# Which of sixteen states ScalarE, VectorE and GpSimd multiply in a selective scan

## The chip, the cores and the metric

The kernel runs on one core of a Trainium2 chip. The metric is the device time of one execution in microseconds (us), the median of several runs.

## The reference

A convolution and state-space block (layer 0) is followed by attention and a mixture of experts with eight experts (layer 1). Only the scan of layer 0 matters here. For each of two images, four groups of channels and four directions of reading the image (K), with D = 128 channels and N = 16 states on L = 2304 positions:

```
dA = exp(d[..., None] * A)
h = h * dA + (d * u)[..., None] * Bv[:, :, None, :]
y = einsum('bkdn,bkn->bkd', h, Cv)
```

So for each state n the kernel needs, for 128 channels by all positions, the decay exp(d*A_n), the drive du*B_n (B_n is one row, the same for all channels), the recurrence along the positions, and the sum over n of h_n*C_n.

## The kernel before, in words

The phases run one after the other; the scan is `scan_phase` (from L587). The 128 channels lie on the partitions and the positions in the free dimension, in chunks of 768 (WC). There are 8 units (image and group); each has 12 steps (4 directions by 3 chunks), and each step has 16 tiles, one for each state n. Every engine has a program written out by hand for the 192 tiles of a unit, in order of t = 16*step + n; the units 1 to 6 run in a hardware loop. Nothing plans the order at run time: an engine takes its instructions in the order of its program and waits on semaphores.

What happens to the tile of state n:

- The decay is one ScalarE exponential (L834), into a buffer `da` (four of them) in SBUF, for the two soft states into PSUM.
- The drive du*B_n is made in one of three ways, by the list in which n stands. For HARD states TensorE spreads the row B_n over all partitions with two matmuls into PSUM (`spread`, L726), and VectorE multiplies this in place with du (`multiply`, L856). For WARM states ScalarE makes the product: du lies transposed (positions on the partitions), so B_n is a scalar of each partition, and six ACTIVATEs of 128x128 with a scale do it (`heat`, L795, into one of two buffers `warm`); TensorE turns the six blocks back into PSUM (`turn`, L734). For SOFT states (4 and 12) GpSimd multiplies du with a copy of B_n that a DMA has put on all partitions (`drive`, L906).
- VectorE runs the recurrence (`scan`, L877); it carries the state in `h[n]` from step to step.
- GpSimd multiplies h with C_n, which a DMA has put on all partitions (`weigh`, L912, six buffers `hc`), and TensorE adds it up over n in PSUM by two matmuls with the identity, which the profile records as four (`sum_up`, L743), eight tiles behind. ScalarE copies the finished y (L778), and the SP queue stores it.

Three PSUM tiles (`ps_p`, PR = 3) go round in order of place. Sixteen places are for the tiles, and a seventeenth, ahead of state 10 (FLIP), is for the flip: six transposes of the next step's du (L715) and six of its `rows`, the B (L717), which ScalarE copies out (`read_flip`, L785) at n = 11. A place is free when the tile three places earlier has been scanned (for the flip: has been copied); `slot_free` waits for that at the start of every flip, spread and turn, and before the exponential of a soft state. Since the flip has a place of its own, tile 10 waits for the scan of tile 8, 11 for 9, and 13 for 10 (12 takes the flip's place); the other tiles wait for the tile three states earlier.

The orders of the programs around the change: TensorE at t takes the flip (if n = 10), then spread or turn of tile t, then the sum of tile t - 8; the sum of state 0 waits for the copy of y. VectorE at t takes the multiply of tile t if it is HARD, then the scan of tile t - 1. ScalarE at t takes the copy of y (n = 9), `read_flip` (n = 11), then the products of tile t + 2 if that is WARM (`HEAT` = 2), then the exponential of tile t. GpSimd takes the drive three tiles ahead, then the product with C of tile t, which waits for the sum six tiles back. The SP queue issues the loads of the next step at n = 8, between the loads of C, and these are paced by GpSimd's products (six buffers).

The lists themselves are four lines at the top of the file:

```
SOFT = (4, 12)
WARM = (1, 3, 6, 8, 10, 13, 15)
HARD = tuple(n for n in range(N) if n not in SOFT + WARM)
FLIP, HEAT = 10, 2
```

Of the kernel before, what the change touches and what calls it, by code (L numbers as in the profile page):

```python
# [29 lines left out]
STACK = 128  # L30
PIECE = 512
SOFT = (4, 12)
WARM = (1, 3, 6, 8, 10, 13, 15)
HARD = tuple(n for n in range(N) if n not in SOFT + WARM)
NB = WC // 128
FLIP, HEAT = 10, 2
# [550 lines left out]
def scan_phase(nc, P, keep):  # L587
# [3 lines left out]
    with ExitStack() as ctx:  # L591
# [21 lines left out]
        TILES = STEP * N  # L613
        NH, NS, NW = STEP * len(HARD), STEP * len(SOFT), STEP * len(WARM)
        steps = [(p + 2 * r, (NCH - 1 - c if r else c), c == 0, r) for p in range(PAIRS) for r in range(2) for c in range(NCH)]
        hard_at = lambda t: (t // N) * len(HARD) + sum(n in HARD for n in range(t % N))
        soft_at = lambda t: (t // N) * len(SOFT) + sum(n in SOFT for n in range(t % N))
        warm_at = lambda t: (t // N) * len(WARM) + sum(n in WARM for n in range(t % N))
        cool_at = lambda t: t - soft_at(t)
# [80 lines left out]
        def _(pe):  # L700
# [19 lines left out]
            def spread(u, t, first, last):  # L720
                st, n = divmod(t, N)
                if n == 0:
                    pe.wait_ge(dd_here[st % 2], u * (48 * STEP // 2) + 48 * (st // 2) + 48)
                slot_free(u, place(t), first, last)
                for lo, hi in pieces:
                    mm = pe.matmul(ps_p[place(t) % PR][:, lo:hi], keep["b_sel"][:, n, :], cut[st % 2][:, lo:hi], start=True, stop=True)  # L726
                mm.then_inc(spread_done, 1)

            def turn(u, t, first, last):
                slot_free(u, place(t), first, last)  # L730
                w = warm_at(t)
                pe.wait_ge(warm_done, u * NW + w + 1)
                for b in range(NB):
                    mm = pe.transpose(ps_p[place(t) % PR][:, b * 128:b * 128 + 128], warm[w % WR][:, b, :], keep["ident"][:, :])  # L734
                mm.then_inc(turned_done, 1)
# [10 lines left out]
            def unit(u, first, last):  # L746
                for t in range(TILES):
# [6 lines left out]
                    if t % N in HARD:  # L754
                        spread(u, t, first, last)
                    elif t % N in WARM:
                        turn(u, t, first, last)
# [16 lines left out]
        def _(act):  # L774
# [5 lines left out]
            def read_flip(u, st, first):  # L780
                act.wait_ge(flip_full, u * STEP + st + 1)
                if not first or st > 1:
                    act.wait_ge(warm_done, u * NW + (st - 1) * len(WARM))
                place = flip_place(st - 1) if st else flip_place(STEP - 1) - STEP * (N + 1)
# [14 lines left out]
            def unit(u, first, last):  # L799
                for t in range(TILES):  # L800
# [14 lines left out]
                    ahead = t + HEAT  # L815
                    if ahead % N in WARM:
                        if ahead < TILES:
# [1121 lines left out]
```

## Time and profile before

| what | value |
|---|---|
| median of 3 runs | 6382.03 us (6374.76 to 6386.11) |
| profiled execution | 6374.7 us, span 6372.7 us |
| TensorE busy, whole span | 5243.1 us (82%) |
| VectorE busy | 4366.0 us (69%) |
| GpSimd busy | 4197.2 us (66%) |
| ScalarE busy | 3768.5 us (59%) |
| scan (806 to 4120 us) | 3314 us |
| granted clock of TensorE | 0.919 over the span |

Shares of the whole span mix the phases: in the profile's 40 slices VectorE, TensorE and GpSimd stand at 8 or 9 tenths in the scan and fall off behind it, where TensorE alone is busy. The rest of the work is best read in stretches. The chain that ended last, as the page gives it, only covers the experts at the end and says nothing of the scan. Durations in the timelines are those of the records; instructions of one engine overlap by some 0.1 us, so the distance from start to start is the time that one takes from its engine. In the timelines DVE is VectorE, ACT ScalarE, POOL GpSimd, PE TensorE's matmuls, PEld its weight loads and SPq the queue of DMA issues on SP.

### The profile page before, as it was taken

The numbers are of one execution on the slowest core, as the hardware profiler recorded it, in microseconds if no ns is written. First come the engines' busy times: TensorE is split into PE (matmuls) and PEld (weight loads), VectorE is DVE, ScalarE is ACT, GpSimd is POOL, SyncE is SP. The second block draws the span as 40 slices with busy tenths as digits, with TensorE's granted clock in tenths as the row PEclk, the third lists the DMA queues.
The fourth block names the chain that finished last, engine by engine and source line by source line (L and its number), as shares of the span: only waits on it lengthen the run. The fifth ranks groups of instructions, "written<-read, shape, count | busy, mean of one in ns | idle before, by whom it ended". The sixth has DMA issues, their size and how long they took to land. (4 is left out here: it accounts for less than half of the span.)

```text
span 6372.7 us, 85894 instructions
## 1 busy us (share of the span) xinstructions
PE 5243.1 (82%) x22476; PEld 3559.1 (56%) x22476; DVE 4366.0 (69%) x4451; ACT 3768.5 (59%) x8015; POOL 4197.2 (66%) x2811
## 2 busy tenths in 40 slices
PE   4767489999898998998989999845699999956994
PEld 2333255555555555555555555422389999935773
DVE  2566599999999999999999999865231111154332
ACT  2555578788777887877878788635532222232332
POOL 0455689999998999999999999831034444402441
PEclk8888599999999999999999999967799999975996
DMA  3454477777777777777777777664200000012213
GB/s 90 139 188 177 186 238 249 249 241 249 240 248 243 238 248 236 249 249 239 248 236 249 249 243 249 221 220 159 72 3 0 0 0 0 0 52 90 84 58 109
DMA packets 399677, 1073.47 MB, mean 168 GB/s; under 512 B 51470, under 2 KB 94511, under 8 KB 393600
## 3 DMA queue, kind: packets, MB, share of 16 engines
q1 hardware_dynamic: 387808, 1043.07, 49.6%
q0 software_dynamic: 7584, 20.72, 1.0%
q10 hardware_dynamic: 3840, 4.72, 0.3%
q8 instruction: 160, 2.62, 0.2%
q14 instruction: 285, 2.33, 0.1%
HBM read 883.39 MB, written 184.94 MB: 168 GB/s over the span
## 5 line engine op out<-in xcount | busy, mean ns | idle before, releaser
L912 POOL TENSOR_TENSOR scan_hc<-scan_h,scan_c_rep 128x768 f32<-128x768 f32 x1536 | 2743.3, 1826 | 259.7 <-PE scan_ps_y L743 233.5
L743 PE MATMUL scan_ps_y<-scan_hc,keep_ident 128*128 128x512 f32 (+1 forms) x6144 | 2220.8, 489 | 24.4 <-ACT scan_y L778 21.0
L877 DVE TENSOR_TENSOR_SCAN scan_h<-scan_da,scan_h,scan_ps_p 128x768 f32<-128x768 f32 x896 | 1572.8, 1793 | 0.0
L743 PEld LDWEIGHTS scan_ps_y<-scan_hc,keep_ident 128*128 128x128 f32 x6144 | 1067.9, 190 | 827.7 <-issue 744.1
L834 ACT ACTIVATE scan_da<-scan_dd,layer_a_neg 128x768 f32<-128x768 f32 x1344 | 1208.8, 925 | 186.5 <-DVE scan_h L877 180.3
L795 ACT ACTIVATE scan_warm<-scan_du_t 128x128 f32<-128x128 f32 x4032 | 1243.1, 388 | 2.7 <-PE scan_ps_p L734 2.3
L1254 POOL TENSOR_TENSOR attn_e_lo<-attn_e,attn_e_hi 128x384 fp32r<-128x384 f32 x432 | 437.1, 1012 | 769.0 <-DVE attn_e_hi L1245 769.0
L877 DVE TENSOR_TENSOR_SCAN scan_h<-scan_da,scan_ps_p 128x768 f32<-128x768 f32 x448 | 760.7, 1733 | 2.0 <-ACT scan_da L834 2.0
L856 DVE TENSOR_TENSOR scan_ps_p<-scan_ps_p,scan_dd 128x768 f32<-128x768 f32 x672 | 634.1, 944 | 138.6 <-PE scan_ps_p L726 137.6
L1245 DVE CAST attn_e_hi<-attn_e 128x384 fp32r<-128x384 f32 x432 | 165.3, 383 | 713.4 <-ACT attn_e L1233 713.4
L734 PE MATMUL scan_ps_p<-keep_ident,scan_warm 128*128 128x128 f32 x4032 | 580.2, 281 | 68.4 <-DVE scan_h L877 64.6
L1233 ACT ACTIVATE attn_e<-attn_ps_s 128x384 f32<-128x384 f32 x432 | 212.6, 492 | 692.7 <-PE attn_ps_s L71 692.7
L734 PEld LDWEIGHTS scan_ps_p<-keep_ident,scan_warm 128*128 128x128 f32 x4032 | 444.5, 142 | 212.3 <-issue 136.0
L726 PE MATMUL scan_ps_p<-scan_cut,layer_b_sel 128*128 128x512 f32 x1344 | 433.5, 404 | 155.3 <-DVE scan_h L877 153.2
L726 PEld LDWEIGHTS scan_ps_p<-scan_cut,layer_b_sel 128*128 128x128 f32 x1344 | 218.6, 190 | 338.0 <-DVE scan_h L877 309.6
L906 POOL TENSOR_TENSOR scan_bu<-scan_dd,scan_b_rep 128x768 f32<-128x768 f32 x192 | 350.1, 1824 | 0.0
L567 POOL TENSOR_TENSOR delta_de<-delta_de,delta_du 128x768 f32<-128x768 f32 x96 | 173.2, 1811 | 261.0 <-ACT delta_du L482 261.0
L69 PE MATMUL attn_ps_s<-f_hi,f_lo 128*128 x864 | 293.1, 339 | 2.1 <-DVE attn_t_lo L1241 2.1
L69 PE MATMUL attn_ps_o<-attn_e_hi,attn_t_lo 128*128 128x384 f32 x864 | 291.5, 337 | 3.7 <-POOL attn_e_lo L1254 3.6
L71 PE MATMUL attn_ps_s<-f_hi 128*128 x864 | 293.0, 339 | 0.0
L70 PE MATMUL attn_ps_s<-f_lo,f_hi 128*128 x864 | 291.6, 338 | 0.0
L71 PE MATMUL attn_ps_o<-attn_e_hi,attn_t_hi 128*128 128x384 f32 x864 | 291.6, 337 | 0.0
(285 smaller groups left out, 7375.6 us busy)
## 6 DMA issues: line engine op xcount, KB each, us to landing
scan_c_rep<-bc_dram SPq DMA_DIRECT2D x1536, 384.0 KB, 4.2
scan_dd<-dd_dram SPq DMA_DIRECT2D x96, 768.0 KB, 5.6
scan_b_rep<-bc_dram SPq DMA_DIRECT2D x192, 384.0 KB, 4.9
dd_dram<-delta_de SPq DMA_DIRECT2D x96, 384.0 KB, 6.7
dd_dram<-delta_du SPq DMA_DIRECT2D x96, 384.0 KB, 7.3
y_dram<-scan_y SPq DMA_DIRECT2D x96, 384.0 KB, 4.7
merge_y<-y_dram SPq DMA_DIRECT2D x32, 1152.0 KB, 10.6
delta_img<-xn_dram SPq DMA_DIRECT2D x16, 576.0 KB, 9.7
```

What stands on the lines that cost most here:

```text
L69: pe.matmul(out, wl, xh, start=start, stop=False)
L71: return pe.matmul(out, wh, xh, start=False, stop=stop)
L726: mm = pe.matmul(ps_p[place(t) % PR][:, lo:hi], keep["b_sel"][:, n, :], cut[st % 2][:, lo:hi], start=True, stop=True)
L734: mm = pe.transpose(ps_p[place(t) % PR][:, b * 128:b * 128 + 128], warm[w % WR][:, b, :], keep["ident"][:, :])
L743: mm = pe.matmul(ps_y[:, lo:hi], keep["ident"][:, :], hc[t % HR][:, lo:hi], start=n == 0, stop=n == N - 1)
L795: last = act.activation(warm[w % WR][:, b, :], du_t[st % 2][:, b * 128:b * 128 + 128], ACT.Identity, scale=du_t[st % 2][:, at:at + 1])
L834: act.activation(dst, dd[st % 2][:, 0, :], ACT.Exp, scale=keep["a_neg"][:, k, n:n + 1]).then_inc(ex_done, 1)
L856: dve.tensor_tensor(x, x, dd[st % 2][:, 1, :], ALU.mult).then_inc(mult_done, 1)
L877: dve.tensor_tensor_scan(view(h[n]), view(x), view(y), start, ALU.mult, ALU.add).then_inc(scan_done, 1)
L906: pool.tensor_tensor(bu[f % SR][:, :], dd[st % 2][:, 1, :], b_rep[f % SR][:, :], ALU.mult).then_inc(bu_done, 1)
L912: pool.tensor_tensor(hc[t % HR][:, :], h[t % N][:, :], c_rep[t % CR][:, :], ALU.mult).then_inc(hc_done, 1)
L1254: pool.tensor_tensor(e_lo[j % 4][:, :], e[j % 4][:, :], e_hi[j % 4][:, :].bitcast(F32), ALU.subtract).then_inc(lo_done, 1)
```

## The change

One list is replaced. States 5, 7, 9 and 11 go from HARD to WARM, and 6, 8 and 10 from WARM to HARD; SOFT and all code stay as they are. Before, a step has 7 HARD, 7 WARM and 2 SOFT states, after it 6, 8 and 2. HARD is (0, 2, 5, 7, 9, 11, 14) before and (0, 2, 6, 8, 10, 14) after.

```diff
-WARM = (1, 3, 6, 8, 10, 13, 15)
+WARM = (1, 3, 5, 7, 9, 11, 13, 15)
```

## Rows read from the trace of the kernel before

**Rows 1.** The scan: us; PE, PEld, DVE, ACT, POOL busy (instructions); clock; DMA share; GB/s
```profile
806.00:4120.00 3314.00, 2992.20 (x12638) 1812.65 (x12638) 3181.06 (x2208) 2645.46 (x5758) 3071.40 (x1726) 0.99 0.75 244
```

**Rows 2.** Waits in the scan: who waited for whom: us, times, longest
```profile
DVE scan_ps_p L856 <- PE scan_ps_p L726: 137.6, 106, 9.9
...
POOL scan_hc L912 <- PE scan_ps_y L743: 233.5, 110, 5.8
...
PE scan_ps_p L715 <- DMA scan_rows<-bc_dram: 74.4, 79, 3.7
```

**Rows 3.** Groups by line; busy us, mean ns, then idle before and releaser
```profile
L795 ACT ACTIVATE scan_warm<-scan_du_t 128x128 f32<-128x128 f32 x4032 | 1243.1, 388 | 2.7 <-PE scan_ps_p L734 2.3
```

**Rows 4.** Timeline of VectorE: start us, us, operation, count, [idle before, releaser]
```profile
2003.41 0.94 DVE L856 TENSOR_TENSOR scan_ps_p<-scan_ps_p,scan_dd 128x768 f32<-128x768 f32 x1
...
2026.49 0.94 DVE L856 TENSOR_TENSOR scan_ps_p<-scan_ps_p,scan_dd 128x768 f32<-128x768 f32 x1
2027.34 3.50 DVE L877 TENSOR_TENSOR_SCAN scan_h<-scan_da,scan_h,scan_ps_p 128x768 f32<-128x768 f32 x2
2031.82 0.97 DVE L856 TENSOR_TENSOR scan_ps_p<-scan_ps_p,scan_dd 128x768 f32<-128x768 f32 x1 [0.98 <-PE scan_ps_p L726]
2032.69 3.51 DVE L877 TENSOR_TENSOR_SCAN scan_h<-scan_da,scan_h,scan_ps_p 128x768 f32<-128x768 f32 x2
2036.12 1.79 DVE L877 TENSOR_TENSOR_SCAN scan_h<-scan_ps_p,scan_h,scan_bu 128x768 f32<-128x768 f32 x1
2037.83 0.94 DVE L856 TENSOR_TENSOR scan_ps_p<-scan_ps_p,scan_dd 128x768 f32<-128x768 f32 x1
...
2074.39 0.97 DVE L856 TENSOR_TENSOR scan_ps_p<-scan_ps_p,scan_dd 128x768 f32<-128x768 f32 x1 [6.83 <-PE scan_ps_p L726]
2075.27 3.39 DVE L877 TENSOR_TENSOR_SCAN scan_h<-scan_da,scan_ps_p 128x768 f32<-128x768 f32 x2
```

**Rows 5.** Timeline of TensorE's matmuls, same columns
```profile
2002.56 1.45 PE L743 MATMUL scan_ps_y<-scan_hc,keep_ident 128*128 128x512 f32 x4
2003.85 0.82 PE L734 MATMUL scan_ps_p<-keep_ident,scan_warm 128*128 128x128 f32 x6
2004.50 1.46 PE L743 MATMUL scan_ps_y<-scan_hc,keep_ident 128*128 128x512 f32 x4
...
2027.21 0.87 PE L715 MATMUL scan_ps_p<-keep_ident,scan_dd 128*128 128x128 f32 x6 [0.38 <-DMA scan_rows<-bc_dram]
...
2029.27 0.87 PE L734 MATMUL scan_ps_p<-keep_ident,scan_warm 128*128 128x128 f32 x6 [0.72 <-DVE scan_h L877]
2029.98 1.46 PE L743 MATMUL scan_ps_y<-scan_hc,keep_ident 128*128 128x512 f32 x4
2031.09 0.70 PE L726 MATMUL scan_ps_p<-scan_cut,layer_b_sel 128*128 128x512 f32 x2
2031.62 2.74 PE L743 MATMUL scan_ps_y<-scan_hc,keep_ident 128*128 128x512 f32 x8
2034.63 0.87 PE L734 MATMUL scan_ps_p<-keep_ident,scan_warm 128*128 128x128 f32 x6 [0.27 <-DVE scan_h L877]
...
2036.44 0.70 PE L726 MATMUL scan_ps_p<-scan_cut,layer_b_sel 128*128 128x512 f32 x2
...
2069.62 1.54 PE L734 MATMUL scan_ps_p<-keep_ident,scan_warm 128*128 128x128 f32 x6
```

**Rows 6.** Timeline of ScalarE, the copy of the flip and the six products behind it
```profile
2028.67 0.89 ACT L785 ACTIVATE scan_du_t<-scan_ps_p 128x864 f32<-128x864 f32 x1 [2.83 <-PE scan_ps_p L717]
2029.45 1.85 ACT L795 ACTIVATE scan_warm<-scan_du_t 128x128 f32<-128x128 f32 x6
```

**Rows 7.** Timeline of GpSimd and of the DMA issues
```profile
2016.73 12.47 POOL L912 TENSOR_TENSOR scan_hc<-scan_h,scan_c_rep 128x768 f32<-128x768 f32 x7
...
2020.31 0.37 SPq L636 DMA_DIRECT2D scan_rows<-bc_dram  x1
...
2031.61 1.81 POOL L912 TENSOR_TENSOR scan_hc<-scan_h,scan_c_rep 128x768 f32<-128x768 f32 x1 [2.40 <-PE scan_ps_y L743]
```

## The prediction

> **What bounds the kernel now.** I read the busy shares by stretch first. The scan runs from about 806 to 4120 us of the span, 3314 us for 96 steps of 16 states (8 units of 12 steps). In it VectorE is busy 3181 us (96%), GpSimd 3071 (93%), TensorE 2992 (90%) and ScalarE 2645 (80%) [rows 1]. Three engines stand within 6% of each other, so shares don't settle it, and the waits come next. VectorE waits for hardly anything but L726, the spread of B by TensorE: 137.6 us. GpSimd waits 233.5 us for TensorE's sums, so it has slack, 2.4 us a step. TensorE waits 74.4 us for the transfer of `rows` [rows 2]. The timeline of one plain step shows the pattern (names: m for the multiply of L856, s for the scan of L877, with the state's number). VectorE takes m14 at 2003.41 and the next m14 at 2037.83: 34.42 us a step. In between it is idle once, 0.98 us ahead of m11 [rows 4]. A multiply takes 0.85 us from start to start (2026.49 to 2027.34), a scan 1.715 (two from 2032.69 to 2036.12) [rows 4]; 16 x 1.715 + 7 x 0.85 = 33.39, and 1.05 from the bubble make 34.44. So VectorE sets the step, with one bubble that TensorE gives it.
>
> The bubble is a chain through three PSUM slots. The flip of du and B for the next step takes a slot ahead of state 10, so that state 11 must wait for the slot of state 9, not 8, and state 10 for that of 8. In the trace: s8 ends at 2029.05 (2027.34 + 1.71); TensorE turns state 10 at 2029.27, sums at 2029.98, spreads state 11 at 2031.09 [rows 5], and m11 starts at 2031.82 [rows 4]: 2.77 us after s8, where VectorE came free after 1.715 (s9).
>
> **The change part by part.** (1) VectorE loses one multiply of seven a step: 0.85 us, 81.6 us over 96 steps, if nothing else moves. This is the whole direct gain.
>
> (2) TensorE loses a spread (two matmuls) and gains a turn (six transposes) a step. From start to start a spread costs 0.53 us (2031.09 to 2031.62), a turn 0.71 (2029.27 to 2029.98) or 0.65 behind other work (2003.85 to 2004.50) [rows 5]. That is +0.2 us on an engine with some 3 us of idle time a step [rows 1]. As a total it is hidden; as a place in a chain it is not (4).
>
> (3) ScalarE gains six ACTIVATEs, 388 ns each by their mean [rows 3], from start to start 1.76 us for six (2029.45 to 2031.21) [rows 6]. Its busy time in the scan goes from 27.6 us a step to 29.4, of 34. I followed its order with these durations: after the change it reaches the copy of y (L778) at about the time at which TensorE's last sum of the step before is there, as now, with two heats and five exponentials between the soft exponential of state 4 and the copy, before and after. So nothing on the path for it; bounds: nothing, and 0.13 us a step (12 us) if the copy slips and takes the flip with it. It has 1.7 us in hand for state 13's product: read_flip would be done 0.8 us after the flip, six ACTIVATEs later is early for turn 13.
>
> (4) The multiplies move from states 0, 2, 5, 7, 9, 11, 14 to 0, 2, 6, 8, 10, 14. This is what I weigh most. I lay VectorE's step out anew: m8 s7 s8 m10 s9 s10 s11 s12 m14 s13 s14 m0.
> First bubble: spread 10 needs the slot of state 8, so it starts 0.14 us after s8 (the same lag as other spreads) and m10 0.73 later: 0.87 instead of 1.05 us. A gain of 0.18. Condition: the flip has ended by then. It starts when s7 is over, takes 1.4 us, and s8 gives 1.715, so it has about 0.4 us to spare, where the order of before leaves 1.3 (m9 and turn 10 lie there too).
> Second bubble, new: turn 11 has to wait for the slot of state 9, and everything behind it on TensorE waits too. Chain from the end of s9: 0.21 to turn 11 (as after s10, whose end is 2032.69 + 1.71 = 2034.40, to turn 13 at 2034.63, [rows 4, 5]), 0.71 for it, two sums (those of t = 11 and of the soft state 12) 2 x 1.28 = 2.56 (a sum is 1.29 start to start, 2002.56 to 2003.85), turn 13 0.65, the sum behind it until spread 14 starts 1.10 (as 2029.98 to 2031.09), and 0.73 to m14: 5.96 us. VectorE has s10, s11 and s12 in that time, 5.15 us, and then stands at m14: 0.82 us. Before the change the spread of 11 came first and m11 itself lay on VectorE, so that spread 14 (2036.44) was ready 0.66 us ahead of m14 (2037.83) [rows 4, 5]. Bounds: none at all, if the sums run closer than I read them, and 1.1 us if turn 11 starts later. In the four steps of twelve where a scan starts from nought, two scans take 3.39 us (2075.27) instead of 3.51 [rows 4], some 1.65 from start to start; there the second bubble is 5.96 - 4.95 = 1.0 us and the one of before 2.77 - 1.65 = 1.12.
> Around states 3, 4 and 5, where no multiply stands any more between m2 and m6, the same chain (6.2 us from s0) has 7.7 us of VectorE's work; no bubble.
>
> (5) The transfers. GpSimd starts the product of state 8 when the sum behind the flip is done (2031.61), works 12 operations through at 1.78 us (12.47 us for 7) = 21.4 us up to the end of state 1's; the SP queue issues `rows` 1.8 us later (2020.31) and the flip starts 8.7 us after that product's end (2027.21) [rows 5, 7]. The new step would need it, relative to the same product, 1.0 us later than now (0.82 of it from the second bubble). So the 0.9 us that the flip loses of its cover it gets back: no cost; bounds below. Closed into a loop this chain is 21.4 + 8.7 + 1.4 + 0.5 + 1.6 = 33.6 us: no step can be shorter than that.
> (6) The loop's edges, where VectorE is idle 6.83 us (2074.39) [rows 4] because `rows` comes late: I count no change. Bounds, 1 us each way on seven of them.
>
> **Sum.** A plain step: -0.85 - 0.18 + 0.82 = -0.21 us; a fresh one: -0.85 - 0.25 + 1.0 = -0.10; mean -0.17, times 96 = -16 us. Nothing outside of the scan changes. The profiled execution took 6374.7 us (span 6372.7, 2 us around it) and would become 6358; it lies 7 us below the median of the runs, 6382, so for a median I say 6366. About 0.2% (13 us) is what a measurement can tell from no change; this is just above it.
>
> **Rivals.** A: the second bubble isn't there (0 instead of 0.82), since sums and turns overlap more than their starts show. Then 32.54 + 0.87 = 33.4 us a step, held up to 33.6 by the loop of (5): 0.8 us less than 34.4, -77 us: 6305. For it: TensorE has 10% idle time [rows 1]. Against: every link is a start-to-start time of the same instructions.
> B, slower: `rows` lands too late. TensorE waits 74.4 us for it, 79 times, 0.9 us each [rows 2], and harmlessly, because the flip has 1.3 us of cover. With 0.4 us of cover and no shift of the issue, 0.6 us more of each bubble would show: +0.6 - 0.2 = +0.4 us a step, +38 us: 6420. It makes the kernel slower from 0.2 us a step. Against: (5), the issue moves ahead with the second bubble.
> C: TensorE's clock. It is granted at 0.99 over the scan [rows 1], 2.4 GHz; at the loop's edge, where TensorE had stood 3.7 us for `rows` [rows 2], six transposes took 1.54 us (2069.62) instead of 0.87, as at the 1.2 GHz level [rows 5]. The change adds an idle stretch of 1.7 us ahead of turn 11. If that brought the lower level in each step, the matmuls in the chain of (4), 5.0 us, would take up to twice as long; half of that, 2.5 us a step, is 240 us: 6620. The many short waits of now (0.72 us ahead of 2029.27) have left the share at 0.99; 2%.
> The Trainium skill, TensorE: Matmul & The Clock Gate, section "A second HAM failure mode: psum-queue depth-cycling", says that many short idle stretches between groups of matmuls can make the clock swing between its levels; by that rule C would be the forecast. The trace of this kernel, which cycles three PSUM slots with a wait at most of them, stays at 0.99, so I don't follow it.
>
> **Chances and range.** Forecast 0.63, A 0.15, B 0.20, C 0.02. The forecast's own range is 6350 to 6385 (0.82 +/- 0.2 us a step is +/- 19 us), about half of it or a little more beyond 0.2%. So faster 0.50 (0.35 and A), same 0.28, slower 0.22 (B and C). Range 6310 to 6396: it leaves out the full size of A and B.
>
> **What would show it.** Multiplies: 576 instead of 672, ACTIVATEs of L795 4608 instead of 4032. In a plain step VectorE has two idle places, ahead of m10 (near 0.8 us in the record, the busy end of the scan before covering 0.08) and ahead of m14 (near 0.75), both released by L726; the step is 34.2 us. VectorE's wait for L726 rises from 137.6 to about 200 us. Wrong: one idle place alone (A), a first one of 1.4 us or more with TensorE waiting for `rows` ahead of it (B), the granted clock under 0.95 (C), or VectorE waiting for ScalarE at L834 or L795's product, which I hold out.

## The result and the profile after

| | before | after |
|---|---|---|
| median of 9 runs each | 6383.54 us (6374.76 to 6389.39) | 6364.78 us (6355.28 to 6374.31) |
| ratio | | 0.9978, 95% interval 0.9969 to 0.9987 |
| profiled execution | 6374.7 us, span 6372.7 | span 6358.2 us |
| start of the first multiply to start of the last group of scans | 806.68 to 4115.22 | 806.09 to 4093.44 |

The change makes the kernel 19 us faster, 0.22%. VectorE lost 96 multiplies worth 82 us. The profile's head and its first part (busy time of each engine) after:

```profile
span 6358.2 us, 87285 instructions
...
PE 5222.5 (82%) x22860; PEld 3620.2 (57%) x22860; DVE 4292.1 (68%) x4355; ACT 3922.1 (62%) x8591; POOL 4214.9 (66%) x2811
```

The same stretch as [rows 1], the scan, which is now 3292 us long instead of 3314 (columns as there):

```profile
806.00:4104.00 3298.00, 2971.49 (x13036) 1874.59 (x13037) 3109.31 (x2112) 2798.38 (x6332) 3085.16 (x1728) 0.99 0.76 245
```

VectorE is less busy by 72 us and yet the scan is only some 21 us shorter: the rest has become idle time. The waits in the scan (who waited for whom: us, times, longest) answer to [rows 2]:

```profile
DVE scan_ps_p L856 <- PE scan_ps_p L726: 185.0, 201, 9.9
POOL scan_hc L912 <- PE scan_ps_y L743: 176.7, 122, 4.0
...
PE scan_ps_p L715 <- DMA scan_rows<-bc_dram: 21.8, 38, 2.1
```

VectorE's wait for the spread went from 106 times and 137.6 us to 201 times and 185.0 us: there are two bubbles a step where there was one. TensorE's wait for `rows` fell from 74.4 to 21.8 us. The two groups of instructions that the change moves (busy us, mean ns, then idle before) answer to [rows 3]:

```profile
L795 ACT ACTIVATE scan_warm<-scan_du_t 128x128 f32<-128x128 f32 x4608 | 1423.8, 388 | 40.4 <-PE scan_ps_p L734 34.7
...
L856 DVE TENSOR_TENSOR scan_ps_p<-scan_ps_p,scan_dd 128x768 f32<-128x768 f32 x576 | 546.8, 949 | 186.2 <-PE scan_ps_p L726 185.0 <-issue 1.2
```

ScalarE has 576 more ACTIVATEs of unchanged length, VectorE 96 fewer multiplies. Now the step itself, in the timelines (start us, us, engine, line, operation, count, idle before and what ended it), as [rows 4]. VectorE from one m14 to the next:

```profile
1999.38 0.97 DVE L856 TENSOR_TENSOR scan_ps_p<-scan_ps_p,scan_dd 128x768 f32<-128x768 f32 x1 [0.80 <-PE scan_ps_p L726]
...
2020.77 3.50 DVE L877 TENSOR_TENSOR_SCAN scan_h<-scan_da,scan_h,scan_ps_p 128x768 f32<-128x768 f32 x2
2024.98 0.97 DVE L856 TENSOR_TENSOR scan_ps_p<-scan_ps_p,scan_dd 128x768 f32<-128x768 f32 x1 [0.71 <-PE scan_ps_p L726]
2025.86 5.21 DVE L877 TENSOR_TENSOR_SCAN scan_h<-scan_da,scan_h,scan_ps_p 128x768 f32<-128x768 f32 x3
2030.98 1.79 DVE L877 TENSOR_TENSOR_SCAN scan_h<-scan_ps_p,scan_h,scan_bu 128x768 f32<-128x768 f32 x1
2033.58 0.97 DVE L856 TENSOR_TENSOR scan_ps_p<-scan_ps_p,scan_dd 128x768 f32<-128x768 f32 x1 [0.80 <-PE scan_ps_p L726]
```

From 1999.38 to 2033.58 it is 34.20 us instead of 34.42. The bubble of 0.71 us is ahead of m10, that of 0.80 ahead of m14. TensorE in the same step, as [rows 5]: the flip, spread 10 and its sum, turn 11 after a wait of 1.56 us, two sums in one row, turn 13, its sum, spread 14.

```profile
2022.97 0.87 PE L715 MATMUL scan_ps_p<-keep_ident,scan_dd 128*128 128x128 f32 x6 [0.29 <-DMA scan_rows<-bc_dram]
...
2024.33 0.62 PE L726 MATMUL scan_ps_p<-scan_cut,layer_b_sel 128*128 128x512 f32 x2
2024.78 1.45 PE L743 MATMUL scan_ps_y<-scan_hc,keep_ident 128*128 128x512 f32 x4
2027.79 0.87 PE L734 MATMUL scan_ps_p<-keep_ident,scan_warm 128*128 128x128 f32 x6 [1.56 <-DVE scan_h L877]
2028.50 2.75 PE L743 MATMUL scan_ps_y<-scan_hc,keep_ident 128*128 128x512 f32 x8
2031.08 0.82 PE L734 MATMUL scan_ps_p<-keep_ident,scan_warm 128*128 128x128 f32 x6
2031.74 1.46 PE L743 MATMUL scan_ps_y<-scan_hc,keep_ident 128*128 128x512 f32 x4
2032.84 0.70 PE L726 MATMUL scan_ps_p<-scan_cut,layer_b_sel 128*128 128x512 f32 x2
```

From turn 11 to spread 14 it takes 5.05 us and 0.74 more to m14. And GpSimd, as [rows 7]: it stands for 1.74 us behind the flip, where it stood for 2.40.

```profile
2012.01 12.65 POOL L912 TENSOR_TENSOR scan_hc<-scan_h,scan_c_rep 128x768 f32<-128x768 f32 x7
2026.41 1.82 POOL L912 TENSOR_TENSOR scan_hc<-scan_h,scan_c_rep 128x768 f32<-128x768 f32 x1 [1.74 <-PE scan_ps_y L743]
```

Taking VectorE's scan of state 12 as a mark in every step, the 95 distances add up to 3256.2 us, before to 3277.5. Six of them, from unit 1 to unit 7, hold an edge at which VectorE waits: 225.7 us now, 231.9 before. The other 89 give 14.9 us, 0.17 us each. Outside of the scan the profiled execution after is 7 us longer than that of before. No instruction there was changed. This part (the span less the time from VectorE's first scan to its last) is 3062 us before and 3069 after, and 3063 to 3077 in the profiled executions of the ten experiments, none of which touches it either, so the 7 us can't be put down to the change.

### The profile page after: what moved, and what is told of

Read it like the earlier page. It is cut to its first block and busy times, and to the rows that moved or that the text cites. A ratio compares the mean times of both kernels' runs of the same rounds, so it can differ in the third digit from the quotient of the medians.

```text
span 6358.2 us, 87285 instructions
## 1 busy us (share of the span) xinstructions
PE 5222.5 (82%) x22860; PEld 3620.2 (57%) x22860; DVE 4292.1 (68%) x4355; ACT 3922.1 (62%) x8591; POOL 4214.9 (66%) x2811
## 5 line engine op out<-in xcount | busy, mean ns | idle before, releaser
L743 PE MATMUL scan_ps_y<-scan_hc,keep_ident 128*128 128x512 f32 (+1 forms) x6144 | 2219.5, 489 | 23.6 <-ACT scan_y L778 23.2
L795 ACT ACTIVATE scan_warm<-scan_du_t 128x128 f32<-128x128 f32 x4608 | 1423.8, 388 | 40.4 <-PE scan_ps_p L734 34.7
L834 ACT ACTIVATE scan_da<-scan_dd,layer_a_neg 128x768 f32<-128x768 f32 x1344 | 1184.5, 922 | 5.5 <-issue 2.8
L734 PE MATMUL scan_ps_p<-keep_ident,scan_warm 128*128 128x128 f32 x4608 | 647.4, 277 | 221.9 <-DVE scan_h L877 221.0
L734 PEld LDWEIGHTS scan_ps_p<-keep_ident,scan_warm 128*128 128x128 f32 x4608 | 532.6, 142 | 372.0 <-issue 162.4
L856 DVE TENSOR_TENSOR scan_ps_p<-scan_ps_p,scan_dd 128x768 f32<-128x768 f32 x576 | 546.8, 949 | 186.2 <-PE scan_ps_p L726 185.0
L726 PE MATMUL scan_ps_p<-scan_cut,layer_b_sel 128*128 128x512 f32 (+1 forms) x1152 | 381.1, 412 | 59.1 <-DVE scan_h L877 44.3
L906 POOL TENSOR_TENSOR scan_bu<-scan_dd,scan_b_rep 128x768 f32<-128x768 f32 x192 | 348.5, 1815 | 0.0
L834 ACT ACTIVATE scan_ps_p<-scan_dd,layer_a_neg 128x768 f32<-128x768 f32 x192 | 172.2, 897 | 273.7 <-DVE scan_h L877 273.7
```

The source lines that it names most:

```text
L743: mm = pe.matmul(ps_y[:, lo:hi], keep["ident"][:, :], hc[t % HR][:, lo:hi], start=n == 0, stop=n == N - 1)
L795: last = act.activation(warm[w % WR][:, b, :], du_t[st % 2][:, b * 128:b * 128 + 128], ACT.Identity, scale=du_t[st % 2][:, at:at + 1])
L834: act.activation(dst, dd[st % 2][:, 0, :], ACT.Exp, scale=keep["a_neg"][:, k, n:n + 1]).then_inc(ex_done, 1)
L856: dve.tensor_tensor(x, x, dd[st % 2][:, 1, :], ALU.mult).then_inc(mult_done, 1)
L906: pool.tensor_tensor(bu[f % SR][:, :], dd[st % 2][:, 1, :], b_rep[f % SR][:, :], ALU.mult).then_inc(bu_done, 1)
```

## The experiments

Theory: what VectorE's list gives or loses is decided by the bubbles that chains through the three PSUM slots leave on it; a second limit lies close by, the loop from GpSimd's product over the load of `rows`, the flip and a sum back to GpSimd. Rivals: the engines' totals decide (TensorE 90% busy, ScalarE's new work, GpSimd), or the transfer does. Ratios are to the kernel before, run on the same chip; the steps named are those of the profiled execution, and an edge is the passage from one unit to the next. The experiments start from the changed kernel, where nothing else is said.

### The sum ahead of turn 11

```diff
+SUM_FIRST = 11
...
+                    if t % N == SUM_FIRST:
+                        sum_up(u, t - BEHIND)
                     if t % N in HARD:
                         spread(u, t, first, last)
                     elif t % N in WARM:
                         turn(u, t, first, last)
-                    if t >= BEHIND:
+                    if t % N == SUM_FIRST:
+                        pass
+                    elif t >= BEHIND:
                         sum_up(u, t - BEHIND)
```

> The changed kernel, with TensorE's sum of t = 11 put ahead of the turn of state 11 instead of behind it. Same instructions on every engine. Theory (two bubbles, each a chain through three PSUM slots): the sum fills the wait of 1.6 us ahead of that turn and leaves the chain to m14, which shrinks from 5.96 to 4.7 us against 5.15 us of VectorE's work: the second bubble goes (0.80/0.98 us in 96 steps, some 82 us of idle time). What remains is held by the loop GpSimd's product, load of rows, flip, sum: 33.6 to 33.9 us a step. So 0.3 to 0.6 us a step less than the changed kernel, 30 to 58 us: 6307 to 6335. Rival (the step is set by the engines' totals, TensorE 90% busy, or by ScalarE's extra work): as the changed kernel, 6365.

Measured: 6320.99 us, ratio 0.9909 (0.9895 to 0.9923), 0.7% below that of the change. VectorE's idle times in three steps, all ahead of m10 (the multiply is L861 here):

```profile
2117.96 0.97 DVE L861 TENSOR_TENSOR scan_ps_p<-scan_ps_p,scan_dd 128x768 f32<-128x768 f32 x1 [1.21 <-PE scan_ps_p L727]
...
2151.30 0.97 DVE L861 TENSOR_TENSOR scan_ps_p<-scan_ps_p,scan_dd 128x768 f32<-128x768 f32 x1 [1.31 <-PE scan_ps_p L727]
...
2184.80 0.97 DVE L861 TENSOR_TENSOR scan_ps_p<-scan_ps_p,scan_dd 128x768 f32<-128x768 f32 x1 [1.34 <-PE scan_ps_p L727]
```

The bubble ahead of m14 is gone, without an instruction more or fewer on any engine. So it was a matter of order, and the rival of the totals falls. But the first bubble has grown from 0.71 to 1.2 or 1.3 us, and the steps take 33.6 us in the mean away from the edges, where slots alone allow 33.0 (the run with early loads below): with the second bubble gone, `rows` comes too late (TensorE waits 70.0 us for it, 78 times).

### State 11 added to the list before

```diff
-WARM = (1, 3, 5, 7, 9, 11, 13, 15)
+WARM = (1, 3, 6, 8, 10, 11, 13, 15)
```

The edit is made on the kernel before; the loads and the order of the sums stay.

> Eight states at ScalarE as in the changed kernel, but the list before with state 11 added: WARM = (1, 3, 6, 8, 10, 11, 13, 15), HARD = (0, 2, 5, 7, 9, 14). Every engine's total is that of the changed kernel. Theory: m11 was where the bubble of before stood; no multiply stands within two states of the flip any more, and one bubble is left, at m14, of about 1.04 us (0.22 + 0.71 + 1.28 + 0.65 + 2.56 + 0.65 + 1.10 + 0.73 = 7.9 us from the end of s8 against four scans, 6.86 us). That makes 33.6 us a step; the loop through GpSimd and the load of rows, with a turn in it, may hold it up to 33.9 or 34.2. Forecast 33.8: 35 us less than the changed kernel, 6330 (6300 to 6360). Rival (totals alone): 6365.

Measured: 6370.89 us, ratio 0.9984 (0.9975 to 0.9993): a miss, by 41 us. VectorE's idle times, the first two in one step:

```profile
2107.19 1.81 DVE L877 TENSOR_TENSOR_SCAN scan_h<-scan_da,scan_h,scan_ps_p 128x768 f32<-128x768 f32 x1 [1.09 <-ACT scan_da L834]
2109.32 1.82 DVE L877 TENSOR_TENSOR_SCAN scan_h<-scan_ps_p,scan_h,scan_bu 128x768 f32<-128x768 f32 x1 [0.32 <-POOL scan_bu L906]
...
2140.81 1.81 DVE L877 TENSOR_TENSOR_SCAN scan_h<-scan_da,scan_h,scan_ps_p 128x768 f32<-128x768 f32 x1 [0.53 <-ACT scan_da L834]
...
2208.55 1.81 DVE L877 TENSOR_TENSOR_SCAN scan_h<-scan_da,scan_h,scan_ps_p 128x768 f32<-128x768 f32 x1 [1.34 <-PE scan_ps_p L734]
```

Hardly any multiply waits any more (m14 does in 9 steps); scans do. Scan 11 waits for its exponential (L834), scan 12 for GpSimd's product (L906), others for the turn (L734). The shortest plain steps took 33.4 to 33.6 us, as I had it, but 21 of 95 took 35 us or more (5 of them at an edge), with TensorE waiting 118.1 us for `rows`. In 15 of the other 16 the granted clock fell to the 1.2 GHz level: at 1302.12, for instance, the flip starts after a wait of 2.24 us for `rows`, and the six transposes of the turn behind it, at 1303.54, take 1.54 us; the clock from 1303 to 1307 is 0.57. The steps with such a stretch take 35.9 us in the mean, the others away from the edges 33.7. How much of the 2.2 us is the clock and how much the wait itself isn't shown.

### The loads of the next step one state later

```diff
-                    if n == 8 and not (first and st == 0):
+                    if n == 9 and not (first and st == 0):
```

> The changed kernel with the loads of the next step issued one state later on the SP queue (n = 9 instead of 8), which is one product of GpSimd, 1.78 us. Theory of the second limit: the loop GpSimd's product, load, flip, spread, sum has some 0.3 us to spare in the changed kernel; 1.78 us more must show by about 1.3 to 1.5 us a step, all in the first bubble (0.71 becomes about 2.1), 125 to 145 us: 6490 to 6510. If the transfer has cover (rival: only the slots count), no change: 6365.

Measured: 6660.58 us, ratio 1.0437 (1.042 to 1.0453), twice the price expected; the steps take 37.5 us in the median, not 35.5. In one step, TensorE's flip after its wait for `rows`, and m10 behind it:

```profile
2095.79 1.54 PE L715 MATMUL scan_ps_p<-keep_ident,scan_dd 128*128 128x128 f32 x6 [3.54 <-DMA scan_rows<-bc_dram]
...
2099.05 0.97 DVE L856 TENSOR_TENSOR scan_ps_p<-scan_ps_p,scan_dd 128x768 f32<-128x768 f32 x1 [5.17 <-PE scan_ps_p L726]
```

The transposes of the flip take 1.54 us, in the row of before 0.87 [rows 5]. The stretches of 10 us around them (us, then busy time of PE, PEld, DVE, ACT, POOL, granted clock, DMA share, GB/s):

```profile
2080.00:2090.00 10.00, 8.85 (x36) 5.15 (x35) 10.00 (x8) 9.75 (x23) 10.00 (x7) 1.00 0.74 213
2090.00:2100.00 10.00, 6.46 (x28) 4.54 (x27) 4.83 (x5) 3.98 (x9) 4.93 (x3) 0.73 0.84 285
2100.00:2110.00 10.00, 9.69 (x41) 5.98 (x41) 9.30 (x7) 9.59 (x23) 8.30 (x5) 0.93 0.47 149
```

The granted clock is 0.73 in the stretch of the wait and 1.00 ahead of it: TensorE had stood for 3.54 us, and then ran at the 1.2 GHz level; a turn at 2101.86 takes 0.87 us again. So the loop is real, 1.78 us later is paid in full, and a wait for `rows` of that length has a second price, the clock (0.889 over the whole span, where the change has 0.917). The steps of this trace divide the 3.3 us: away from the edges 76 of 89 hold a stretch at the lower level and take 37.5 us in the mean, and the 13 without one take 35.8, near the 35.5 expected. So about half goes with the clock; this compares steps that also differ in their waits, and no run has the wait without the clock. The changed kernel itself keeps 0.99 over the scan.

### The loads two states earlier

```diff
-                    if n == 8 and not (first and st == 0):
+                    if n == 6 and not (first and st == 0):
```

> The changed kernel with the loads of the next step issued two states earlier (n = 6). Theory: the floors of both bubbles (0.71, and 0.80 or 0.98 us) are made by slots and not by the transfer, so they stay; only the irregular part goes. Recorded idle time of VectorE in the scan is 178.8 us, the floors make 149 of it: at most 30 us, I say 15: 6350. If the transfer sets the step instead (rival B of the prediction), the first bubble shrinks in every step, by 0.3 us or more, 30 us or more beyond that: under 6330.

Measured: 6344.09 us, ratio 0.9944 (0.993 to 0.9957), 0.34% below the change. VectorE's idle times of two steps:

```profile
2126.44 0.97 DVE L856 TENSOR_TENSOR scan_ps_p<-scan_ps_p,scan_dd 128x768 f32<-128x768 f32 x1 [0.71 <-PE scan_ps_p L726]
...
2135.04 0.97 DVE L856 TENSOR_TENSOR scan_ps_p<-scan_ps_p,scan_dd 128x768 f32<-128x768 f32 x1 [0.80 <-PE scan_ps_p L726]
...
2160.10 0.97 DVE L856 TENSOR_TENSOR scan_ps_p<-scan_ps_p,scan_dd 128x768 f32<-128x768 f32 x1 [0.71 <-PE scan_ps_p L726]
...
2168.64 0.97 DVE L856 TENSOR_TENSOR scan_ps_p<-scan_ps_p,scan_dd 128x768 f32<-128x768 f32 x1 [0.98 <-PE scan_ps_p L726]
```

0.71 and 0.80 (0.98 in the fresh step) are unchanged, and now they are so in every step: away from the edges, the 89 distances are 34.1, 34.2 and 33.5 us in turn. TensorE waits for `rows` nowhere. So the floors are the slots', and rival B of the prediction isn't the limit of a usual step; the transfer costs the irregular rest only, here 0.34%.

### The same on the kernel before

The edit is that of the last experiment, on the kernel before.

> The kernel before, with nothing but the loads of the next step two states earlier (n = 6). In the changed kernel that made every step regular. Theory: the bubble ahead of m11 (0.97 us) is made by slots and stays, the irregular part goes, so about as much as there, 15 to 20 us: 6360 to 6365; and the change made on top of it (this kernel against the changed one with early loads, 0.9944 of the kernel before) is worth 0.2 us a step, 19 us, as on the record: this kernel's ratio about 0.997. Rival (the change hid or cost something at the transfers): the two with early loads lie closer than 8 us or further than 35 us apart.

Measured: 6363.66 us, ratio 0.9974 (0.9963 to 0.9984). Its steps are 34.2, 34.4 and 33.8 us in turn. Against 34.1, 34.2 and 33.5 with the change, that is 0.54 us in three steps before rounding, 0.18 us a step; by the ratios (0.9944 and 0.9974) 0.3%, 19 us. The gain of the change does not come from the transfers.

### Early loads and the sum ahead of turn 11

The first and the fourth edit together.

> Changed kernel with early loads (n = 6) and the sum of t = 11 ahead of the turn of state 11. With late rows no longer in the way, the second bubble should go and nothing come in its place: 0.88 us in 64 steps and 1.05 in 32, 90 us less than with early loads alone: ratio about 0.980 to the kernel before (6250 to 6265), 33.3 us a plain step, one idle place of 0.71 us a step. Rival (something else then holds the step, GpSimd or ScalarE): 0.985 or more, other idle places.

Measured: 6257.19 us, ratio 0.981 (0.9796 to 0.9825). One idle place a step is left, ahead of m10:

```profile
2122.28 0.96 DVE L861 TENSOR_TENSOR scan_ps_p<-scan_ps_p,scan_dd 128x768 f32<-128x768 f32 x1 [0.71 <-PE scan_ps_p L727]
...
2155.14 0.97 DVE L861 TENSOR_TENSOR scan_ps_p<-scan_ps_p,scan_dd 128x768 f32<-128x768 f32 x1 [0.71 <-PE scan_ps_p L727]
```

The steps are 33.0, 33.3 and 32.6 us in turn, 0.9 to 1.1 less than with early loads alone. The second bubble of the change had a price of 1.3%, six times what the change gained.

### Early loads and state 11 in the list before

The second edit with early loads, on the kernel before.

> WARM = (1, 3, 6, 8, 10, 11, 13, 15) with early loads. Without them its plain steps took 33.5 us but many were thrown out to 35 or 36 us, with waits for rows, for the exponential of 11 and for GpSimd's drive of 12. Theory: all of these follow from late rows, because the flip comes ahead of two turns and of the products of 13. Then every step takes 33.5 us (33.0 fresh): 0.6 us less than with early loads alone, 58 us: ratio 0.985, 6285. Rival (ScalarE's order is the cause, two lots of six ACTIVATEs next to each other): stays near 0.995.

Measured: 6295.65 us, ratio 0.9867 (0.9849 to 0.9886), 10 us above the forecast. Steps of 33.4, 33.6 and 33.1 us away from the edges, with two exceptions, 0.3 and 0.6 us longer. The irregular ones of the run without early loads were the transfer's; but the idle places are still scan 11 and scan 12, not m14:

```profile
2108.69 1.81 DVE L877 TENSOR_TENSOR_SCAN scan_h<-scan_da,scan_h,scan_ps_p 128x768 f32<-128x768 f32 x1 [0.53 <-ACT scan_da L834]
2110.85 1.82 DVE L877 TENSOR_TENSOR_SCAN scan_h<-scan_ps_p,scan_h,scan_bu 128x768 f32<-128x768 f32 x1 [0.35 <-POOL scan_bu L906]
```

Scan 11 waits here because ScalarE comes to its exponential behind the copy of the flip and six ACTIVATEs. My sum for a bubble of 1.04 us at m14 named the wrong place; that the idle time at scans 11 and 12 is of about that size (0.88 us here) is chance, since another chain makes it.

### The flip behind state 10

```diff
-FLIP, HEAT = 10, 2
+FLIP, HEAT = 11, 2
```

with early loads and the sum first.

> Changed kernel with early loads, the sum of t = 11 first, and the flip one place later (FLIP = 11, behind state 10). Theory: m10 then finds its slot (that of state 7) in time and the first bubble goes too; chain from s8: flip, sum, turn 11, sum, turn 13, sum, spread 14, 7.3 us against 7.7 of VectorE's work. No bubble is left: 16 x 1.715 + 6 x 0.85 = 32.5 us a plain step; GpSimd's 18 operations of 1.78 us are 32.1. 80 us less than with the sum first alone: ratio 0.967 to 0.970, 6170 to 6190. Rival: GpSimd and its ring of six buffers hold it at 33 us or more: 0.975 or more.

Measured: 6173.49 us, ratio 0.9678 (0.9664 to 0.9692). This is the fastest version, 3.2% under the kernel before. Its scan (columns as [rows 1]) and its waits:

```profile
806.00:3916.00 3110.00, 2951.62 (x13035) 1858.02 (x13036) 3089.54 (x2113) 2791.42 (x6336) 3073.04 (x1727) 1.00 0.79 261
```

```profile
DVE scan_ps_p L861 <- PE scan_ps_p L727: 14.7, 6, 10.1
POOL scan_hc L917 <- PE scan_ps_y L744: 9.8, 15, 1.9
```

Both bubbles are gone; of the 14.7 us that VectorE still waits for spreads, 10.1 are one wait at the start of the scan. Steps take 32.2, 32.5 and 31.8 us. VectorE and GpSimd are both busy for 99% of the scan, and the granted clock is 1.00.

### State 5 back at VectorE

On the fastest version:

```diff
-WARM = (1, 3, 5, 7, 9, 11, 13, 15)
+WARM = (1, 3, 7, 9, 11, 13, 15)
```

> The kernel with no bubble left (early loads, the sum of t = 11 first, flip behind state 10), with state 5 back at VectorE: WARM = (1, 3, 7, 9, 11, 13, 15), seven multiplies a step as before the change. Both m5 and m6 find their slots in time. Theory: a multiply costs its whole 0.85 us where no bubble hides it, 82 us over 96 steps: 33.4 us a plain step, ratio 0.9805 (6250 to 6260). Rival (GpSimd, 32.1 us a step and 99% busy, sets the step, so that VectorE's work is no longer what counts): under 20 us, ratio under 0.971.

Measured: 6259.25 us, ratio 0.9805 (0.9791 to 0.9818), as expected. This is the direct gain of the change, one multiply fewer a step, measured by itself: 0.0127, 81 us, and 0.86 us a step in the profiled executions. The change brought 19 us of it.

### State 6 at ScalarE too

Again on the fastest version:

```diff
-WARM = (1, 3, 5, 7, 9, 11, 13, 15)
+WARM = (1, 3, 5, 6, 7, 9, 11, 13, 15)
```

> The same kernel with state 6 at ScalarE too: nine products, five multiplies a step (HARD = 0, 2, 8, 10, 14). VectorE would need 31.7 us a plain step, GpSimd's 18 operations need 32.1. The mean of the three kinds of step is 32.17 now. Theory: GpSimd takes over, at most 0.1 us a step is left to gain: same time within 10 us, ratio 0.966 to 0.969, with VectorE idle some 0.7 us a step on waits for GpSimd or TensorE. Rival (GpSimd's ring gives way and VectorE still sets the step): 80 us less, 0.955.

Measured: 6379.96 us, ratio 0.9993 (0.9984 to 1.0002): a miss: 0.0315 above the ratio with eight, 201 us. The waits in the scan:

```profile
PE scan_ps_y L744 <- ACT scan_y L783: 207.6, 95, 2.3
...
DVE scan_ps_p L861 <- PE scan_ps_p L727: 164.8, 123, 9.9
...
DVE scan_h L882 <- POOL scan_hc L917: 37.3, 53, 4.3
```

In one step, the copy of y on ScalarE (L783) and TensorE's sum of state 0 (L744) that waits for it:

```profile
2143.23 0.79 ACT L783 ACTIVATE scan_y<-scan_ps_y 128x768 f32<-128x768 f32 x1
...
2144.07 1.56 PE L744 MATMUL scan_ps_y<-scan_hc,keep_ident 128*128 128x512 f32 x4 [2.17 <-ACT scan_y L783]
```

TensorE waits for this copy in every step (95 times, 2.2 us in the mean), where it waited 0.25 us in the changed kernel (23.2 us, 91 times) and in the version with eight (23.1 us, 92 times). Behind that sum stand all turns and spreads of the next states, and VectorE waits for them again. ScalarE comes late to the copy because the products of 5, 6 and 7 lie in a row ahead of it, and it waits for one of the two buffers to be turned (149.4 us between 1000 and 3900 us of the span); that this alone makes it late is argued, not shown: no run had a third buffer.

The clock has a share of its own. One step earlier the same sum stands behind the same wait; here are this sum, the m10 behind it, and stretches of 4 us at this sum and at the one above (columns as [rows 1]):

```profile
2108.71 2.62 PE L744 MATMUL scan_ps_y<-scan_hc,keep_ident 128*128 128x512 f32 x4 [2.16 <-ACT scan_y L783]
2114.28 0.97 DVE L861 TENSOR_TENSOR scan_ps_p<-scan_ps_p,scan_dd 128x768 f32<-128x768 f32 x1 [2.54 <-PE scan_ps_p L727]
2108.00:2112.00 4.00, 3.29 (x9) 2.08 (x10) 3.74 (x3) 4.00 (x9) 1.63 (x2) 0.63 0.72 239
2144.00:2148.00 4.00, 3.93 (x17) 2.73 (x18) 3.14 (x3) 4.00 (x12) 2.38 (x3) 1.00 0.58 218
```

The sum takes 2.62 us instead of 1.56 and the granted clock is 0.63 instead of 1.00: after 2.16 us without work TensorE runs at the 1.2 GHz level here, and not in the next step. Away from the edges 30 of 89 steps, nearly one in three, hold such a stretch and take 35.2 us in the mean; the other 59 take 33.55, and the version with eight products 32.2, without such a stretch. So of the 1.9 us that a step grew, some 1.4 go with the late copy and its waits alone, and some 0.6 with the clock. This is read from the steps of one trace; no run keeps the clock up with the wait in place.

The theory's price for GpSimd (10 us at most) had left ScalarE's order out; the totals (31.2 us of its work a step by the prediction's numbers) gave no hint of it.

## Why the prediction was right

- The direct gain, 81.6 us, is right: the run with state 5 back at VectorE gave 81 us for it.
- The first bubble moved from m11 to m10 and shrank. The forecast was 0.87 in place of 1.05 from start to start; recorded idle time is 0.71 in place of 0.98 [rows 4], from start to start 2024.98 - 2020.77 - 3.43 = 0.78, with 3.43 for the two scans as in the prediction. So it gained 0.27 instead of 0.18.
- The second bubble came where it was put, ahead of m14, behind the wait of turn 11. Forecast 0.82 and 1.0 us in plain and fresh steps; recorded 0.80 and 0.98, to which the busy end of the scan before adds 0.08. So the second bubble is 0.06 us larger than forecast and the first 0.09 us smaller; the two errors nearly cancel in a step. The chain was priced at 5.96 us from the end of s9 and measures 0.21 + 5.05 + 0.74 = 6.0. That a reordering of one sum takes the whole bubble away (0.9944 to 0.981) shows the cause.
- A plain step was to take 34.2 us and takes 34.20; the mean gain was to be 0.17 us a step and is 0.17.
- No cost at the transfers: right in sign. The shift of the flip against GpSimd's product was right as well, and TensorE's waits for `rows` fell by 53 us. With early loads on both sides the change is worth the same 19 us.
- ScalarE's work hidden: right for eight states; TensorE waits for the copy of y as little as before (23.2 us in all, before 21.0). The experiment with nine shows how little was left: one more lot of six took away the cover.
- The edges gave 6 us, for which I had none; the rest of the span took 7 us more in the profiled execution. These two cancel, and that the span came out at 6358.2 us, against 6358, is luck to that extent. The median fell by 19 us where the profiled executions differ by 14.5, so part of its nearness to the forecast is luck too.
- Rival A (no second bubble) is a different order, not this kernel; its loop of 33.6 us is met by the mean of the run without the second bubble (33.6 us away from the edges) but is no floor for a step, as part (5) had it: that run has steps from 32.6 to 35.0 us. Rival B was the limit of single steps only. Rival C's mechanism exists in this kernel, but not at the 1.56 us ahead of turn 11, where the clock stays. It shows behind waits of 3.54 us (loads one state later), of 2.24 us (state 11 added) and, in one step of three, of 2.2 us (nine products).
- The change adds a stretch of 1.56 us in each step in which TensorE stands, and the granted clock stays at 0.99 over the scan. The rule of the Trainium skill that the prediction weighed under C (TensorE: Matmul & The Clock Gate, "A second HAM failure mode: psum-queue depth-cycling") would have it swing; for the changed kernel the measurement decides against it. In the version with nine products, where the stretch is 2.2 us in each step, the clock does swing as the rule says.

The median came at 6364.78 us, against 6366.

## What to carry to other kernels

Where three engines are within a few per cent of each other, an instruction taken off the busiest is worth its whole duration only if no other engine's in-order program makes a new wait of it; lay the step out once by hand, with the slot that each instruction waits for and all that stands behind it on its engine. The bubble is then cheap to remove by order (a sum put ahead of a waiting turn, a flip one place later, a load earlier): 3.2% here, against 0.2% for the shift of work. And after one limit falls, ask for the next before shifting more: the ninth state cost all that had been won, in part by a wait that got long enough to lower TensorE's clock. When a run misses, compare the steps with and without a stretch of low clock before giving the whole loss to the wait.

## What the runs showed of the hardware

- A wait of TensorE of 3.54 us for a transfer was followed by transposes at 1.54 us for six instead of 0.87 and a granted clock of 0.73 over 10 us; waits of 1.56 us in every step left it at 0.99. Waits of 2.2 us in every step were followed by the lower level in 30 of 89 steps (0.98 over the scan, transposes again at 1.49 us for six at 2111.12). One state later for a load cost 4.6% for that reason among others.
- Six ACTIVATEs of 128x128 kept their mean of 388 ns when there were 576 more of them, and GpSimd's 18 operations a step ran at 99% busy next to VectorE at 99% with hardly longer durations (the product with C: 1833 ns in the mean, 1826 before).
